# A linear-attention block's first phase: relu written over the projection in its PSUM bank, and v's high part moved ahead of the reading of the first column sums

## The reference, cut to what matters

```python
x = conv(x)                                   # a 128x128 circulant inverse over channels, 16 images
t = tokens(x)                                 # 16 batches x 1024 tokens x 128 channels
n = layernorm(t)
Q, K = elu(n @ Wq.T) + 1, elu(n @ Wk.T) + 1   # 8 heads of 16
V = n @ Wv.T
t = t + (causal linear attention of Q, K, V, divided by its denominator) @ Wout.T
t = t + gated_ffn(layernorm(t))               # the second phase
```

## Time and profile before

| | us |
|---|---|
| median of 3 runs | 846.81 (846.75 to 847.09) |
| the profiled execution | 848.7 |
| its span | 846.9 |
| PE busy | 739.7 (87%) |
| DVE busy | 742.6 (88%) |
| ACT busy | 670.2 (79%) |
| POOL busy | 534.6 (63%) |

### The profile page before, as it was taken

How to read it: one execution, slowest core, us unless ns; L and a number is a source line. 1 busy time by engine, 2 the same in 40 slices (tenths; PEclk the granted TensorE clock), 3 DMA queues, 4 the chain that set the end, 5 groups by cost and what they waited for, 6 DMA issues and landing times. The chain is left out here.

```text
span 846.9 us, 37199 instructions
## 1 busy us (share of the span) xinstructions
PE 739.7 (87%) x11168; PEld 538.4 (64%) x11168; DVE 742.6 (88%) x2736; ACT 670.2 (79%) x1875; POOL 534.6 (63%) x1009
## 2 busy tenths in 40 slices
PE   1588999999999999999999999968899998899994
PEld 1255666666666666666666666648577777577773
DVE  6587999999999999999999999955788985689894
ACT  1477898999989989998898988844788885688884
POOL 5486888888888888888988988810133342033333
PEclk9888999999999999999999999977999999999998
DMA  2255444454444444544454444410022221122222
GB/s 80 52 126 118 98 111 105 92 117 109 91 111 106 105 105 100 116 106 99 106 111 95 116 100 98 88 33 26 2 77 86 77 74 51 38 64 76 74 87 75
DMA packets 165473, 74.10 MB, mean 87 GB/s; under 512 B 139212, under 2 KB 152687, under 8 KB 165368
## 3 DMA queue, kind: packets, MB, share of 16 engines
q1 hardware_dynamic: 165432, 73.58, 36.0%
HBM read 22.69 MB, written 17.30 MB: 47 GB/s over the span
## 5 line engine op out<-in xcount | busy, mean ns | idle before, releaser
L795 DVE SCALAR_TENSOR_TENSOR scores_lo<-p_a,scores_hi 128x512 f16<-128x512 f32 x256 | 164.0, 682 | 0.0
L698 ACT ACTIVATE scores_hi<-p_a 128x512 f16<-128x512 f32 x256 | 138.5, 600 | 6.4 <-PE p_a L543 6.2
L861 POOL TENSOR_TENSOR stats<-stats,consts 128x1 f32<-128x1 f32 x128 | 78.1, 610 | 75.7 <-DVE stats L745 75.6
L1312 POOL TENSOR_TENSOR ffn_rstd_shift<-ffn_rstd_shift,consts 128x4 f32<-128x4 f32 x32 | 36.7, 1146 | 132.8 <-DVE ffn_rstd_shift L1271 132.8
L886 POOL TENSOR_TENSOR qk_parts<-qk_f,qk_parts 128x128 f16<-128x128 f32 x256 | 104.9, 429 | 0.1
L867 POOL TENSOR_TENSOR stats<-stats,consts 128x1 f32<-128x1 f32 x128 | 89.0, 695 | 18.7 <-DVE stats L751 17.1
L560 PE MATMUL p_o<-v_parts,scores_hi 128*128 128x17 f16 x1024 | 90.2, 171 | 12.1 <-ACT scores_hi L698 6.2
L560 PEld LDWEIGHTS p_o<-v_parts,scores_hi 128*128 128x128 f16 x1024 | 80.4, 96 | 30.0 <-issue 27.6
L1095 PE MATMUL psb<-merged_W_of_batch,h_hi 128*128 128x128 f16 x512 | 94.2, 220 | 4.9 <-DVE h_lo L1249 3.8
L1249 DVE TENSOR_TENSOR h_lo<-h_f,h_hi 128x512 f16<-128x512 f32 x128 | 95.0, 782 | 1.2 <-ACT h_hi L1152 1.2
L1141 ACT ACTIVATE h_f<-psb,merged_b_of_batch 128x512 f32<-128x512 f32 x128 | 87.0, 711 | 11.4 <-PE psb L1076 11.3
(11 more groups left out here) (195 smaller groups left out, 3009.6 us busy)
## 6 DMA issues: line engine op xcount, KB each, us to landing
x_f<-in_x SPq DMA_DIRECT2D x32, 256.0 KB, 2.9
t_rows<-t SPq DMA_DIRECT2D x64, 128.0 KB, 1.9
t_back<-t_rows SPq DMA_DIRECT2D x32, 256.0 KB, 2.6
out<-out_tile SPq DMA_DIRECT2D x32, 256.0 KB, 2.0
tv_share<-in_L_ffn_tv_W SPq DMA_DIRECT2D x32, 128.0 KB, 2.2
qkT_parts<-qk_parts SPq DMA_TRANSPOSE x128, 3.1
base_ffn_weights<-in_L_ffn_W SPq DMA_DIRECT2D x2, 256.0 KB, 4.3
W_hi_lo_rows<-base_parts SPq DMA_DIRECT2D x4, 128.0 KB, 3.8
```

The lines of the kernel that those rows point to most:

```text
L698: nc.scalar.activation(ah[:, t % 2, cols], p_a[:, cols], ACT.Relu).then_inc(ahi_ready[eo], 1)
L795: nc.vector.scalar_tensor_tensor(al[:, t % 2, cols], p_a[:, cols], 0.0, ah[:, t % 2, cols], ALU.max, ALU.subtract).then_inc(alo_ready[eo], 1)
```

## The change

Four edits, all in the first phase. `relu_qk` writes its result over its own input in `p_in`, not into a tile of its own in SBUF. It now waits for `exp_qk`, which has to have read that input, and ACT does `exp_qk` before `relu_qk`. `make_qk` reads exp from SBUF and relu from the PSUM bank, and also waits for `v_hi`, which reads the same bank. ACT does `v_hi` ahead of `read_t1`. `project`, and the first work after the loop on PE, wait for `make_qk` and not for exp and relu.

```diff
-SCALAR_ORDER = [("split_x", 0), ("relu_qk", 1), ("exp_qk", 1), ("read_t1", 6), ("v_hi", 1), ("z_hi", 8),
+SCALAR_ORDER = [("split_x", 0), ("exp_qk", 1), ("relu_qk", 1), ("v_hi", 1), ("read_t1", 6), ("z_hi", 8),
...
-            rq = sb(pa_, "relu_qk", [P, 4, 2 * C])
...
-                        at_least(pe, exp_ready, n - 1)
-                        at_least(pe, relu_ready, n - 1)
+                        at_least(pe, qk_ready, n - 1)
                         at_least(pe, vlo_ready, n - 1)
...
-                    pe.wait_ge(exp_ready, NT)
-                    pe.wait_ge(relu_ready, NT)
+                    pe.wait_ge(qk_ready, NT)
                     pe.wait_ge(vlo_ready, NT)
...
                     def relu_qk(b, t):
                         n = TILES * b + t
-                        act.wait_ge(rstd1, n + 1)
-                        act.wait_ge(in_done, n + 1)
-                        at_least(act, qk_ready, n - 3)
-                        nc.scalar.activation(rq[:, t % 4, :], p_in[:, t % 2, 0:2 * C], ACT.Relu, scale=st[:, t % 4, 8:9])\
-                            .then_inc(relu_ready, 1)
+                        act.wait_ge(exp_ready, n + 1)
+                        x = p_in[:, t % 2, 0:2 * C]
+                        nc.scalar.activation(x, x, ACT.Relu, scale=st[:, t % 4, 8:9]).then_inc(relu_ready, 1)
...
                         dve.wait_ge(exp_ready, n + 1)
                         dve.wait_ge(relu_ready, n + 1)
+                        dve.wait_ge(vhi_ready, n + 1)
                         at_least(dve, lo_ready, n - 3)
-                        nc.vector.scalar_tensor_tensor(qk[:, t % 4, :], eq[:, t % 4, :], 1.0, rq[:, t % 4, :],
+                        nc.vector.scalar_tensor_tensor(qk[:, t % 4, :], eq[:, t % 4, :], 1.0, p_in[:, t % 2, 0:2 * C],
                                                        ALU.min, ALU.add).then_inc(qk_ready, 1)
```

## The result

The changed kernel takes 864.28 us (862.63 to 864.94, 4 runs) against 846.95 for the kernel before in the same comparison: 1.020 of it, 95% interval 1.0182 to 1.0217. That is 2% slower. I had forecast 843.2, and the range ended at 854. The profiled execution took 864.94 us, its span is 863.1.

The account below looks back on a forecast made before the run. DVE was taken to set the pace at 4.045 us a slot; after the change a ring through ACT would, at 4.015, saving 3.6 us over 120 slots: 845.1 profiled, 843.2 predicted for the median, range 834 to 854.

Parts of the forecast that it names:

- Step 1: DVE's make_qk with relu in PSUM: takes 0.42 us without the long form; split slots gain 0.42, plain ones lose 0.04.
- step 4: ACT's v_hi ahead of read_t1, make_qk behind v_hi: make_qk starts 0.29 us late in plain slots, 0.31 in split ones.
- the ring: Cycle of waits from make_qk through q_hi and ACT back, setting the pace: 4.01 us split, 3.89 plain; chance 0.45.
- Step 2: ACT's relu_qk after exp_qk with a wait: 0.47 + 0.04 us from exp's start, 0.14 more on ACT, within its idle time.
- Step 3: ACT's relu_qk writing into PSUM: takes 0.47 us (0.41 to 0.57), with the next start 0.37 later.
- The slower rival: ACT's v_hi does not overlap the end of relu's PSUM write: 0.10 us more, 4.115 a slot, 855 us; chance 0.30.
- the sum: Slot time over both kinds of slot, tv_hi included: 4.015 us against 4.045, saving 3.6 us over 120 slots.
- the hop: From the end of ACT's v_hi to the start of DVE's make_qk: 0.10 us, bounded by 0.04 and 0.15.
- the stretch: From q_hi's start to the start of ACT's exp and relu: 2.21 us in a split slot, 2.08 in a plain one.
- Step 5: PE waits for make_qk and v_lo, not for exp, relu and v_lo: nothing starts earlier or later, worth nothing.

Follow-up runs that it names:

- wait alone: Kernel before with v_hi ahead of read_t1 on ACT and make_qk also waiting for v_hi; relu stays in SBUF, ahead of exp: 851.98 us, 1.006.
- operand back: Changed kernel with relu written to an SBUF tile again and read from there by make_qk; order and waits as changed: 868.49 us, 1.025.
- both shortenings: Changed kernel with ACT order exp, v_hi, relu, and make_qk working out its register value before waiting for relu (attached), v_hi and lo: 830.15 us, 0.980.
- Wait attached: Changed kernel; make_qk works out its register value first, then waits for v_hi (attached), relu and lo, without the exp wait: 845.97 us, 0.999.
- order alone: Kernel before with only v_hi moved ahead of read_t1 on ACT: 842.52 us, 0.995.
- relu waits: Kernel before with exp ahead of relu and relu waiting for exp; result still in SBUF, v_hi in its old place: 846.64 us, 0.9996.
- v_hi between: Changed kernel with ACT's order exp, v_hi, relu and all waits as they are: 833.82 us, 0.985.

## Why the prediction was wrong

Its steps, one by one.

Step 1, `make_qk` at 0.42 with no spread: right (0.421), in part by luck. With both inputs in SBUF it takes 0.426 and 0.425 on the median too, in wait alone and operand back, where it starts behind a wait; and with relu in PSUM and both shortenings, where it mostly does not wait, it goes down to 0.371. So the 0.04 over the short form goes with the wait at least as much as with the operand. And its gain was set against a start at the old time. I had the new start 0.3 later in step 4 and `x_lo`'s end at 306.01 in the earlier trace rows, and did not put the two together: at 305.77 only 0.24 of `x_lo` was left. Wait alone and operand back show it: relu in PSUM is worth 4 us here. For the pace of the ring this made no difference, since the ring counts only the instruction's own length; it made the step look as if it paid for the wait.

Step 2, the wait of relu for exp: right in size (304.10 - 303.61 = 0.49, 308.19 - 307.68 = 0.51). That ACT's idle time covers it holds only outside a ring; it was counted in the ring all the same.

Step 3, relu into PSUM: 0.448 where I took 0.47, and 0.37 to the next start, as taken. The slower rival's mechanism, a `v_hi` that can't overlap relu's write, did not occur, though its side was the right one. The Trainium skill (PSUM — Partial Sum Buffer, section "Specifications (TRN2)") has ScalarE write faster to PSUM than to SBUF; here it is 0.448 us against 0.468, 0.02, and against 0.474 in operand back, where relu has the same wait and writes to SBUF.

Step 4 is the one that failed, and the sum with it. The mechanism was right, and two terms of the ring were too small:

- "behind a wait that is one of four I take 0.10": the hop was 0.21 and 0.22, outside the 0.04 to 0.15 by which I had bounded it. Wait attached, where it is 0.03, gave 18 us back; 0.18 x 120 would be 22, but in one slot of eight the hop is 0.40 in both kernels. My two rows for hops had one wait instruction or none behind the last arrival; this one has two. The range was too narrow by this bound.
- "From the start of `q_hi` to the start of the pair are 304.42 - 302.21 = 2.21 us in a split slot": it was 311.94 - 309.60 = 2.34, and 2.34 in 27 of 36 split slots, 2.52 in the others. It was also the lowest value to be had: in the kernel before it is 2.21 or 2.22 in 10 of 38 split slots and 2.25 to 2.40 in the rest. In the slot that I had read, `q_hi` had started 0.39 after `make_qk`'s end, so ACT was behind and PE ahead of it. In the ring ACT is early, and PE comes last: `v_lo` ends at 310.03, `project` starts at 310.17, `turn_out` at 310.66, `gate`'s last matmul ends at 311.10, `gate_relu` starts at 311.28. That path is read from the trace; no run takes it away.

```profile
310.17 0.32 PE L505 MATMUL p_in<-w_in_hi,x_hi 128*128 128x384 f16 x1 [0.31 <-DVE v_parts L754]
310.66 0.27 PE L576 MATMUL p_m<-consts,attn_out 128*128 128x128 f32 x1
...
310.88 0.22 PE L604 MATMUL p_m<-zT_lo,gate_hi 128*128 x1
```

  In the plain slot the stretch was 307.68 - 305.52 = 2.16 for 2.08. There `rsqrt1`, which hangs on DVE's `eps1`, ended at 307.56, so that the ring may go through the statistics there. But only 9 of the 36 plain slots have 2.16; the others have 2.08 to 2.10, as predicted.

Split slot: 0.12 of hop and 0.13 make the 0.25 between 4.01 and 4.26. Plain slot: 0.11 and 0.08, less 0.02 of step 2, make the 0.18 (rounded) between 3.89 and 4.07. On the mean of all 72 slots, `tv_hi` included, the hop was 0.23 where I had 0.10, and the stretch 2.25 where I had 2.21: 0.13 and 0.04 of the 0.16 between 4.015 and 4.179. So the hop is the term that mattered.

Step 5, PE's other wait, worth nothing: no run tells it apart.

The loss along the row of kernels before, order alone, wait alone, operand back, changed, in us: v_hi ahead -4.7, the wait for `v_hi` +9.5, exp ahead with relu's wait +16.5, relu in PSUM -4.2; 17.1 in all, of 17.3 measured. The total has to come out, since each kernel is the start of the next step, so it proves nothing; and each price holds for its place in the row, as relu waits (0) against the +16.5 shows.

## What to carry to other kernels

When an edit turns an engine that was always busy into one that waits, the sum of work is no longer the measure: write the ring down, with each step read over a whole period of slots (here eight), and where that step had to wait, not where it was late anyway. Then place the instructions of the ring so that a wait of one for another is filled (exp, v_hi, relu), and make the last arrival the wait that is attached to the instruction. And where one engine holds another's instruction, look first whether the order of the holder can be changed: a swap of two POOL stages and one of two ACT stages gave 2.9%, where the four edits around the operand in PSUM cost 2%.

## What the runs showed of the hardware

Where the last arrival stands among an instruction's waits has a price: 0.03 us from the end of the releasing instruction to the start where that wait is the attached one (wait attached), 0.09 where it is in the second of three steps (v_hi between), 0.20 to 0.22 where it is in the first (the changed kernel).

`make_qk` of 256 columns takes 0.370 at its shortest, and 0.42 to 0.43 where it starts behind a wait, with both inputs in SBUF (wait alone) and with one in PSUM (the changed kernel); what makes that 0.05 was not looked into.

`make_qk` with both inputs in SBUF and a POOL instruction of 136 or 256 columns hold each other (0.83 for `make_qk` behind `x_lo`, 0.64 for `state_lo` behind `make_qk`). POOL's one-column `rsqrt2` does not hold `make_qk` (0.38), but is held by it: from 200 to 500 us it takes 0.72 to 0.81 in the 55 of 74 slots of the kernel before in which `make_qk` runs as it starts, or starts up to 0.03 behind it, and 0.55 in the others. In the changed kernel, with an operand of `make_qk` in PSUM, it takes 0.54 to 0.55 in all 72, 27 of them with `make_qk` running as it starts. So that operand freed POOL as well, an engine that had the time anyway.
